# Four edits to a fused transformer kernel: early projections, interleaved scores, dealt experts, one-hots by half rows

## The chip, the cores and the metric

The kernel runs on one core of one Trainium2 chip. The metric is device time in microseconds, from the first to the last instruction of the program on that core. A core has TensorE (matmuls, into PSUM), VectorE, ScalarE and GpSimd (elementwise work), and SyncE, which here only issues DMAs. Each engine runs its own list of instructions in the order in which the kernel wrote it; they meet at semaphores. GpSimd can't read PSUM.

## The reference, cut to what matters

Input x is 4 batches of 512 tokens with 128 features, all float32. Between the parts the tokens are layer-normed.

```python
# layer 0, attention: gated, in groups of 32 tokens, plus a linear term over the batch
normed = layernorm(x)
v, gate = split(silu(normed @ W_h + b_h))          # 256 + 256
qk = silu(normed @ W_qk + b_qk)
quad_q, lin_q, quad_k, lin_k = qk * os_gamma[h] + os_beta[h]      # four scaled copies (as named there)
attn = relu(quad_q @ quad_k.T / 32 + bias) ** 2     # inside groups of 32
out = (gate * (attn @ v + lin_q @ (lin_k.T @ v) / n)) @ W_out + b_out + x
# layer 0, feed-forward: 8 experts of 128x128, the best 2 of them for each token
out = sum(top_w * (x @ We[top_idx]))
# layer 1, attention: 16 heads of 8, softmax features of q and k (16 each), causal
q, k = [softmax(p), softmax(-p)] of the mapped q and k
y = (q * cumsum(k v)) / (q * cumsum(k));  out = y @ w_out.T
# layer 1, feed-forward ("peer"): 8 heads; each token scores 2 x 32 keys a head, takes the best 8 of the
# sums, and mixes 64 of 1024 small experts: sum of sigmoid(score) * gelu(x . down[n]) * up[n]
```

## The kernel before, in words

Tokens stand in tiles of 128 (T = 4 a batch, 16 in all). The program has two parts, `layers` and `peer`.

**`layers`** runs rounds s = 1 to 4. In round s the batch a = s goes through layer 0 (helpers `a_...`) while the batch b = s - 1 goes through layer 1's attention (helpers `b_...`); batch 0's layer 0 stands ahead of the loop, and in round 4 there is only a `b`. Each engine has its own list, written by hand, in its own `for s in range(1, B + 1)` loop. In a round TensorE first projects batch a (`a_val`, `a_qk`, `a_gate`: 128x512 f32 matmuls from `wh` and `wqk`), between them it transposes tiles 2 and 3 of batch b and projects them (`b_x2t(b, 1)`, `b_qkv(b, 1)`); ScalarE takes the silu of queries, gates and values (L365, L383, L389), and the exponentials of layer 1's features (`b_exp`, L443). A change between silu and exp costs a table load. VectorE makes the maxima, sums and quotients of the features (`b_maps`, `b_features` L875 to L877), and GpSimd some scaled copies and differences.

The scores of layer 1 are `b_scores` (L1329): for each tile u and each group g of heads (four groups, each in 32 rows of the array) 8 matmuls of 32 rows and 128 columns, f16, high and low part of the query. A group's scores fill one PSUM bank (banks 4 and 5 in turn; in round 4 four banks), VectorE multiplies them with the causal mask (`b_masked`, L905) and sets the bank free, ScalarE and GpSimd split the product in f16 parts, and `b_numerators` (L1346 to L1363) multiplies them with the values into bank 6 or 7, where `b_summed` (L937) adds them up. Between these stand the experts of batch a: `a_experts` on TensorE (L1250, two matmuls of 128x512 f32 for a tile, each recorded as two instructions) and on VectorE (L842, 8 weighted sums a tile, two tiles in turn).

**`peer`** works on 8 pairs of tiles. Each token of a pair has chosen 64 experts, and their numbers are split in a high part (0 to 7) and a low part (0 to 127). For each pair, choices lie on 128 partitions: 64 of the first tile, 64 of the second; the 128 tokens of a tile are "lanes" on the free axis. `one_hots(p)` on VectorE writes `hot_hi` (L1876: is the high part e?), `hot_w` (L1882: that times the weight, in an f16 high and low part), and `hot_lo` (L1889: is the low part k? for three quarters of the lanes). ScalarE writes the last quarter, `hot_last` (L1746 for each lane, and L1752). `hot_w` has a block for each tile of the pair, and the block of the other tile is zero (a memset at the start, L1677). `gathered(p, q)` on TensorE (L2015) then takes each lane: the low one-hot (128x128) as weights, `hot_w` (16 columns: 2 tiles x 8) as moving data, twice (high and low part), so that both tiles of the pair lie beside each other in PSUM bank 2 + q. `weigh(p)` (L1904) multiplies that with the activations `hid` into `mix`, and scales by 1/4096. `outputs(p)` (L2029) multiplies `mix` with `upw`. Between these TensorE computes key scores for tiles two pairs ahead (`key_scores`, L1968) and the activations of the next batch (`hidden`, L1979; in pairs 2 to 5), and VectorE chooses the best keys (`first_choice` L1815, L1819; `second_choice` L1826, L1829). VectorE's order in a pair: one-hots, statistics of the pair before, second choice, `which_side`, `weigh`, first choice.

## Time and profile before

| | |
|---|---|
| median of 3 timed runs | 570.6 us (570.55 to 571.2) |
| the profiled execution's own time | 572.47 us |
| its span | 570.7 us |
| mean granted TensorE clock | 0.733 |
| busy: VectorE, TensorE, ScalarE, GpSimd | 481.5, 419.4, 307.2, 182.2 us |

The profiled execution is one execution of the program; its span runs from the first to the last recorded instruction. Its rows carry the start (us from the span's start), the length, the engine (PE is TensorE, PEld its weight load, DVE VectorE, ACT ScalarE, POOL GpSimd), the line of the kernel, the operation, and the tiles it writes and reads. In brackets stands for how long the engine had been idle and whom it waited for. `layers` takes the first 314 us or so, its rounds begin at about 67, 130, 192 and 256 us; pair 0 of `peer` writes its one-hots at about 345.

### The profile page before, as it was taken

What the parts mean: (1) busy time and instruction counts of PE and PEld (TensorE: products, weight loads), DVE (VectorE), ACT (ScalarE), POOL (GpSimd) and SP (SyncE); (2) the same over time, 40 slices, a digit from 0 to 9 for tenths busy, and PEclk for the clock granted to TensorE, in tenths of its full rate; (3) what the DMA queues carried; (4) which work ended last, traced back from release to release, by engine and by line L of the source; (5) the groups of instructions that cost most, each with busy time, mean ns of one, the idle gap of its engine ahead of it and who ended that gap; (6) DMA issues with size and microseconds to landing.
All of it is one profiled execution on the core that took longest, in us unless ns stands there. A gap on an engine that the chain in (4) does not pass through costs nothing. (4 is left out here: it accounts for less than half of the span.)

```text
span 570.7 us, 12499 instructions
## 1 busy us (share of the span) xinstructions
PE 419.4 (73%) x4564; PEld 300.4 (53%) x4564; DVE 481.5 (84%) x2076; ACT 307.2 (54%) x639; POOL 182.2 (32%) x208
## 2 busy tenths in 40 slices
PE   1777869987999879965754864756698869784485
PEld 1454547654776457633653323554465555554475
DVE  4485877699887989599894699999999999999991
ACT  0611275426652475313640558483788778786591
POOL 4540122943277143833350330303040404030000
PEclk9997979688867977795555785575757575757577
DMA  7220000000000000000000000000000000000000
GB/s 214 71 59 0 1 2 2 1 2 0 1 1 3 0 2 1 2 1 0 1 2 1 1 1 1 3 1 11 2 11 1 12 2 12 1 11 2 11 2 20
DMA packets 12459, 6.72 MB, mean 12 GB/s; under 512 B 3182, under 2 KB 11758, under 8 KB 12398
## 3 DMA queue, kind: packets, MB, share of 16 engines
q1 hardware_dynamic: 10566, 4.34, 2.8%
q10 hardware_dynamic: 1832, 1.58, 0.9%
q8 instruction: 36, 0.59, 0.4%
q14 instruction: 25, 0.20, 0.1%
HBM read 4.87 MB, written 1.05 MB: 10 GB/s over the span
## 5 line engine op out<-in xcount | busy, mean ns | idle before, releaser
L1746 ACT ACTIVATE hot_last<-iota_f,lo_last 128x128 f16<-128x128 f32 x256 | 77.5, 393 | 0.3 <-DVE lo_last L1872 0.3
L2015 PE MATMUL psum<-hot_w,hot_lo 128*128 128x16 f16 x1536 | 44.3, 174 | 25.1 <-DVE hot_lo L1889 17.9
L2015 PEld LDWEIGHTS psum<-hot_w,hot_lo 128*128 128x128 f16 x1536 | 43.4, 104 | 36.8 <-DVE hot_lo L1889 24.5
L1979 PE MATMUL psum<-x3t,down_t 128*128 128x512 f32 x64 | 45.3, 832 | 16.8 <-ACT hid L1711 15.1
L1889 DVE TENSOR_TENSOR hot_lo<-lo_t,iota_lo 128x4096 f16<-128x4096 f16 x24 | 53.6, 2287 | 0.3
L1659 POOL TENSOR_TENSOR eq<-eq,side_f 128x1024 f16<-128x1024 f16 x14 | 28.9, 2085 | 55.9 <-DVE eq L1850 55.9
L1329 PE MATMUL psum<-q_hi,k_t 32*128 32x128 f16 x256 | 36.1, 259 | 8.9 <-DVE masked L905 7.7
L1667 POOL TENSOR_TENSOR rstd<-rstd,minus_half 128x2 f32<-128x2 f32 x8 | 5.6, 702 | 113.4 <-DVE rstd L1922 113.4
L1819 DVE FIND_INDEX8 side_i<-side,keysims 128x8 uint32<-128x32 f32 x256 | 41.5, 184 | 0.0
L1250 PE MATMUL psum<-we,x1t 128*128 128x512 f32 x64 | 40.2, 777 | 0.4 <-DVE z L842 0.4
L2029 PE MATMUL psum<-upw,mix 128*128 128x128 f32 x256 | 36.9, 306 | 0.0
L584 POOL TENSOR_TENSOR a_rstd<-a_rstd,minus_half 128x2 f32<-128x2 f32 (+1 forms) x12 | 9.6, 803 | 84.6 <-DVE a_rstd L749 84.6
L1329 PE MATMUL psum<-q_lo,k_t 32*128 32x128 f16 x256 | 36.3, 261 | 0.0
L2029 PEld LDWEIGHTS psum<-upw,mix 128*128 128x128 f32 x256 | 36.3, 226 | 0.0
L636 POOL TENSOR_TENSOR s_lo<-masked,s_hi 128x512 f16<-128x512 f32 x28 | 31.7, 1157 | 12.4 <-ACT s_hi L472 8.7
L636 POOL TENSOR_TENSOR s_lo<-feat,s_hi 128x512 f16<-128x512 f32 x28 | 31.6, 1155 | 6.5 <-ACT s_hi L472 6.5
L1968 PE MATMUL psum<-keysim,xn 128*128 128x512 f32 x32 | 30.6, 1056 | 3.4 <-ACT keysims L1704 3.4
L1979 PEld LDWEIGHTS psum<-x3t,down_t 128*128 128x128 f32 x64 | 15.0, 256 | 33.9 <-ACT hid L1711 18.4
L1329 PEld LDWEIGHTS psum<-q_hi,k_t 32*128 32x128 f16 x256 | 24.4, 113 | 15.9 <-DVE masked L905 10.2
L472 ACT CAST s_hi<-masked 128x512 f16<-128x512 f32 x32 | 19.1, 617 | 23.5 <-DVE masked L905 23.5
L905 DVE TENSOR_TENSOR masked<-psum,causal 128x512 f32<-128x512 f32 x32 | 20.4, 683 | 11.7 <-PE psum L1329 11.5
L842 DVE SCALAR_TENSOR_TENSOR z<-psum,wexp,z 128x128 f32<-128x128 f32 x112 | 29.6, 341 | 0.0
(271 smaller groups left out, 1166.8 us busy)
## 6 DMA issues: line engine op xcount, KB each, us to landing
xall<-in_L_attn_x SPq DMA_DIRECT2D x4, 256.0 KB, 6.3
out<-o SPq DMA_DIRECT2D x8, 128.0 KB, 2.3
we<-in_L_ffn_We SPq DMA_DIRECT2D x1, 512.0 KB, 4.4
downn<-in_L_ffn_down SPq DMA_DIRECT2D x1, 512.0 KB, 5.3
upw<-in_L_ffn_up SPq DMA_DIRECT2D x1, 512.0 KB, 6.3
wh<-in_L_attn_W_h SPq DMA_DIRECT2D x1, 256.0 KB, 4.7
keysn<-in_L_ffn_keys_p ACTq DMA_DIRECT2D x1, 256.0 KB, 9.7
wqkv<-in_L_attn_w_qkv ACTq DMA_DIRECT2D x1, 192.0 KB
```

The source lines that it names most:

```text
L636: nc.gpsimd.tensor_tensor(s_lo[:, u % 2, g, :], masked[u % 2][:, g, :], s_hi[:, u % 2, g, :], ALU.subtract).then_inc(slo_ok.h, 1)
L842: ins = nc.vector.scalar_tensor_tensor(z2[:, u, :], src, wexp[:, u, e:e + 1], (z2 if e else x1)[:, u, :], ALU.mult, ALU.add)
L1250: ins = nc.tensor.matmul(bank[Y_BANK[u] + k][:], x1t[:, P * u:P * u + P], v.we[:, 4 * k:4 * k + 4, :].rearrange("p e m -> p (e m)"), start ...
L1329: ins = nc.tensor.matmul(bank[S_BANK[b][g]][:, P * c:P * c + P], k_t[r, u, c, :], q[r, u, c, :], start=(q is q_hi), stop=(q is q_lo))
L1659: nc.gpsimd.tensor_tensor(hit, hit, bc(side_f[:, u % 4].rearrange("p i r h -> p (i r) h").unsqueeze(3), [P, 2 * K, NH, K]), ALU.mult)\
L1746: ins = nc.scalar.activation(hot_last[:, lane], iota_f[:], ACT.Abs, bias=lo_last[:, lane:lane + 1], scale=-1.0)
L1819: ins = nc.vector.max_index(side_i[:, u % 4, s, :], side[:, u % 4, s, :], keysims[:, u % 4, s, :])
L1889: nc.vector.tensor_tensor(hot_lo[:, pairs], bc(lo_t[:, lanes].rearrange("p (j s) -> p j s", s=2).unsqueeze(2), [P, LB // 2, P, 2]), bc(v.i ...
L1968: nc.tensor.matmul(bank[6][:], xn[:, P * (u % T):P * (u % T) + P], v.keysim[:].rearrange("p s k -> p (s k)"), start=True, stop=True)\
L1979: nc.tensor.matmul(bank[H_BANK(b, c)][:], v.down_t[:, c, :], v.x3t[:, N * b:N * b + N], start=True, stop=True).then_inc(h_mm.h, 1)
L2015: ins = nc.tensor.matmul(bank[2 + q][:, c:c + 2 * EH], low, hot_w[:, i, lane // 2, :, :, lane % 2].rearrange("p t e -> p (t e)"), start=(i ...
L2029: ins = nc.tensor.matmul(outputs_of(p, t), mix[:, EH * t + e, :], v.upw[:, e, :], start=False, stop=(e == EH - 1))
```

## The change

Five things are moved or rewritten.

1. The projections of batch a (`a_qk`, `a_gate`, `a_val`) leave the start of round s and stand at the end of round s - 1 (the first ahead of the loop), on TensorE and ScalarE. With them some calls of the round change places: on VectorE the statistics `b_z3_spread` go ahead of `b_features(b, 0)`, `b_low_keys` and `a_attn` ahead of `b_x3`; on GpSimd the two head copies go ahead of a root.
2. `b_scores` computes the groups of a half in turn (as many as there are banks), one matmul of each, and waits for all their banks first.
3. The expert matmuls of tile 1 are dealt between the scores of tiles 2 and 3; the numerators of tile 1 come after those scores. On VectorE the first expert sums go ahead of `b_summed(b, 1)`.
4. `hot_w` has no zero block any more. It is written in two products on all 128 partitions, and `gathered` multiplies the two halves of the partitions separately: 4 matmuls a lane, of 64 rows and 8 columns, the two tiles into two banks. `weigh` is a plain product; the scale goes into `upw`, once, on GpSimd.
5. In `peer` the first key scores stand ahead of the second `hidden`.

```diff
 ScalarE
+                def a_front(b):
+                    a_qk(b)
+                    a_gate(b, 0)
+                    a_val(b, 0)
+                    a_val(b, 1)
+                    a_gate(b, 1)
...
                 act.wait_ge(pads.h, 2)
+                a_front(1)
                 for s in range(1, B + 1):
                     a, b = s, s - 1
                     b_exp(b, 0)
                     b_x2t(b, 1)
                     if a < B:
-                        a_qk(a)
                         a_heads(a)
                     b_maps(b, 1)
-                    b_features(b, 0)
-                    if a < B:
-                        a_val(a, 0)
-                        a_gate(a, 0)
-                        a_val(a, 1)
-                        a_gate(a, 1)
-                    b_exp(b, 1)
                     b_values(b, 1)
                     if a < B:
                         a_link(a)
+                    b_features(b, 0)
                     b_value_head(b)
-                    if b > 0:
-                        b_x3t(b - 1)
+                    b_exp(b, 1)
                     if a < B:
                         a_kv(a)
                     b_value_part(b)
                     b_transposed(b, 0)
+                    if b > 0:
+                        b_x3t(b - 1)
...
                     b_yt(b)
+                    if a + 1 < B:
+                        a_front(a + 1)
 VectorE
-                    b_features(b, 0)
                     if b > 0:
                         b_z3_spread(b - 1)
+                    b_features(b, 0)
                     b_maps(b, 1)
+                    b_low_keys(b, 0)
+                    if a < B:
+                        a_attn(a)
                     if b > 0:
                         b_x3(b - 1)
-                    if a < B:
-                        a_attn(a)
-                    b_low_keys(b, 0)
...
                         b_masked(b, 3)
+                        a_experts(a, 0)
                         b_summed(b, 1)
-                        a_experts(a, 0)
 TensorE
                     for s in range(1, B + 1): ...
-                    if a < B:
-                        a_val(a, 0)
-                        a_qk(a)
-                        a_gate(a, 0)
                     b_x2t(b, 1)
                     if a < B:
-                        a_val(a, 1)
+                        a_link(a)
                     b_qkv(b, 1)
                     if a < B:
-                        a_gate(a, 1)
                         a_sim(a)
-                        a_link(a)
+                        a_kv(a)
+                    b_transposes(b, 0)
+                    if a < B:
+                        a_outt(a, 0)
                     if b > 0:
                         b_x3t(b - 1)
-                    if a < B:
-                        a_kv(a)
-                        a_outt(a, 0)
-                    b_transposes(b, 0)
...
                         b_numerators(b, 0)
                         a_experts(a, 0)
-                        a_experts(a, 1)
                         b_scores(b, 2, (1,))
+                        a_experts(a, 1, (0,))
                         b_scores(b, 3, (0,))
+                        a_experts(a, 1, (1,))
+                        b_scores(b, 3, (1,))
                         b_numerators(b, 1)
-                        b_scores(b, 3, (1,))
                         b_numerators(b, 2)
...
+                    b_yt(b)
+                    if a + 1 < B:
+                        a_qk(a + 1)
                     b_z3(b)
+                    if a + 1 < B:
+                        a_rest(a + 1)          # gate 0, val 0, val 1, gate 1
 b_scores
-                    for g in (2 * i + j for i in halves for j in range(2)):
-                        banks = len(set(S_BANK[b]))
-                        if 4 * u + g >= banks:
-                            wait(pe, masked_ok, b, 4 * u + g - banks + 1)
-                        r = slice(32 * g, 32 * g + 32)
+                    for first in range(0, len(groups), banks):
+                        together = groups[first:first + banks]
+                        if 4 * u + together[-1] >= banks:
+                            wait(pe, masked_ok, b, 4 * u + together[-1] - banks + 1)
                         for c in range(QUADS):
                             for q in (q_hi, q_lo):
+                                for g in together: ...
 peer
-                nc.gpsimd.memset(hot_w[:], 0.0).then_inc(zeroed.h, 1)
...
+                nc.gpsimd.tensor_scalar(v.upw[:], v.upw[:], 1.0 / WEIGHT_SCALE, None, ALU.mult).then_inc(upw_ok.h, 1)
...
-                    for t in range(2):
-                        q = slice(HK * t, HK * t + HK)
-                        for i, w in enumerate((w_hi, w_lo)):
-                            ins = nc.vector.tensor_tensor(
-                                hot_w[q, i, :, t], hot_hi[q],
-                                bc(w[q].rearrange("p (j s) -> p j s", s=2).unsqueeze(2), [HK, P // 2, EH, 2]),
-                                ALU.mult)
+                    for i, w in enumerate((w_hi, w_lo)):
+                        ins = nc.vector.tensor_tensor(
+                            hot_w[:, i], hot_hi[:],
+                            bc(w[:].rearrange("p (j s) -> p j s", s=2).unsqueeze(2), [P, P // 2, EH, 2]), ALU.mult)
...
-                        wait(dve, g_mm, p, q + 1)
+                        wait(dve, g_mm, p, q // 2 * 2 + 2)
...
                         for i in range(2):
-                            c = 2 * EH * (lane % LB)
-                            ins = nc.tensor.matmul(
-                                bank[2 + q][:, c:c + 2 * EH], low,
-                                hot_w[:, i, lane // 2, :, :, lane % 2].rearrange("p t e -> p (t e)"),
-                                start=(i == 0), stop=(i == 1))
+                            for t in range(2):
+                                half, c = slice(HK * t, HK * t + HK), EH * (lane % (2 * LB))
+                                low = hot_lo[half, lane // 2, :, lane % 2] if q < QB - 1 else hot_last[half, lane - LB * q, :]
+                                ins = nc.tensor.matmul(
+                                    bank[2 + q // 2 * 2 + t][:, c:c + EH], low, hot_w[half, i, lane // 2, :, lane % 2],
+                                    start=(lane % (2 * LB) == 0 and i == 0), stop=(i == 1), skip_group_check=True)
...
                 hidden(0, 0)
+                key_scores(0)
                 hidden(0, 1)
-                key_scores(0)
```

## Rows read from the trace of the kernel before

**Rows 1.** The page, busy us, share of the span and instructions of each engine.
```profile
PE 419.4 (73%) x4564; PEld 300.4 (53%) x4564; DVE 481.5 (84%) x2076; ACT 307.2 (54%) x639; POOL 182.2 (32%) x208
```
**Rows 2.** Windows: stretch, its length, PE, PEld, DVE, ACT, POOL busy, clock, DMA.
```profile
455.00:490.00 35.00, 29.53 (x365) 22.07 (x364) 34.51 (x241) 24.38 (x58) 7.54 (x12) 0.63 0.02 6
```
**Rows 3.** The chain that ended last, pair 4 of the last layer: start, us, what.
```profile
461.88 0.61 DVE hot_hi L1876
462.51 1.28 DVE hot_w L1882 x2
...
479.90 2.39 DVE mix L1904 x4
...
491.14 0.61 DVE hot_hi L1876
```
**Rows 4.** VectorE's waits from 95 to 250: for whom, us, times, longest.
```profile
DVE masked L905 <- PE psum L1329: 11.5, 3, 4.2
```
**Rows 5.** Timeline around 170 us, round 2: start, us, engine, line, operation.
```profile
168.08 4.82 PE L1250 MATMUL psum<-we,x1t 128*128 128x512 f32 x8
...
173.55 0.69 DVE L905 TENSOR_TENSOR masked<-psum,causal 128x512 f32<-128x512 f32 x1 [3.43 <-PE psum L1329]
```
**Rows 6.** Groups by line: shapes, count, busy us, mean ns, idle before.
```profile
L905 DVE TENSOR_TENSOR masked<-psum,causal 128x512 f32<-128x512 f32 x32 | 20.4, 683 | 11.7 <-PE psum L1329 11.5
...
L1882 DVE TENSOR_TENSOR hot_w<-hot_hi,w_hi 64x1024 f16<-64x1024 f16 x16 | 11.0, 685 | 0.4
L1882 DVE TENSOR_TENSOR hot_w<-hot_hi,w_lo 64x1024 f16<-64x1024 f16 x16 | 10.9, 679 | 0.0
...
L1876 DVE TENSOR_TENSOR hot_hi<-hi_t,iota_hi 128x1024 f16<-128x1024 f16 x8 | 5.5, 684 | 0.0
```
**Rows 7.** Timeline of VectorE in the last pair.
```profile
559.23 0.69 DVE L1904 SCALAR_TENSOR_TENSOR mix<-psum,hid 128x512 f32<-128x512 f32 x1 [2.08 <-PE psum L2015]
```
**Rows 8.** Timelines of TensorE and VectorE in pair 2.
```profile
420.03 1.86 PE L2015 MATMUL psum<-hot_w,hot_last 128*128 128x16 f16 x64
...
421.28 2.48 DVE L1904 SCALAR_TENSOR_TENSOR mix<-psum,hid 128x512 f32<-128x512 f32 x4
```
**Rows 9.** Timeline of TensorE in pair 4.
```profile
467.94 1.90 PE L2015 MATMUL psum<-hot_w,hot_lo 128*128 128x16 f16 x64
...
475.00 2.06 PE L1968 MATMUL psum<-keysim,xn 128*128 128x512 f32 x2
477.17 1.86 PE L2015 MATMUL psum<-hot_w,hot_last 128*128 128x16 f16 x64
```
**Rows 10.** Timeline of TensorE, scores of groups 0 and 1 in round 1.
```profile
93.31 0.23 PE L1329 MATMUL psum<-q_hi,k_t 32*128 32x128 f16 x1
...
93.54 0.23 PE L1329 MATMUL psum<-q_hi,k_t 32*128 32x128 f16 x2
...
93.95 0.21 PE L1329 MATMUL psum<-q_lo,k_t 32*128 32x128 f16 x1
```
**Rows 11.** Timeline at the start of the last layer.
```profile
314.67 3.75 PE L1979 MATMUL psum<-x3t,down_t 128*128 128x512 f32 x4 [1.68 <-PEq L316]
...
316.47 0.81 ACT L1696 ACTIVATE xn<-x3t,bn_shift,bn_scale 128x512 f32<-128x512 f32 x1 [1.13 <-DVE bn_shift L1935]
...
318.22 1.06 PE L1968 MATMUL psum<-keysim,xn 128*128 128x512 f32 x1
```
**Rows 12.** Groups by line, GpSimd.
```profile
L605 POOL TENSOR_SCALAR heads_t<-qk_t,gam,bet 128x512 f32<-128x512 f32 x8 | 7.7, 968 | 0.1
```
**Rows 13.** Timeline at the start of round 2.
```profile
131.66 1.02 PE L1155 MATMUL psum<-x3t,wh 128*128 128x512 f32 x2
...
132.97 1.06 ACT L443 ACTIVATE pe_in<-pe_in 128x1024 f32<-128x1024 f32 x1 [4.97 <-DVE pe_in L867]
...
134.06 1.22 DVE L875 TENSOR_REDUCE psum_<-pe_in 128x128 f32<-128x1024 f32 x1
...
141.56 1.28 ACT L443 ACT_TABLE_LOAD   x1
```
**Rows 14.** Timeline of VectorE, first query split of round 1.
```profile
87.49 0.69 DVE L893 SCALAR_TENSOR_TENSOR q_lo<-psum,q_hi 128x512 f16<-128x512 f32 x1 [3.00 <-ACT q_hi L463]
```

More of the change, by code:

```diff
@@ L1241, in a_logits, with a_experts @@
                     ins.then_inc(logit_mm.h, 1)
-                def a_experts(b, u):
+                def a_experts(b, u, halves=(0, 1)):
                     if u == 2 and b:
@@ L1248, in a_experts @@
                         wait(pe, y_used, b, 1)
-                    for k in range(2):
+                    for k in halves:
                         ins = nc.tensor.matmul(bank[Y_BANK[u] + k][:], x1t[:, P * u:P * u + P],
@@ L1321, in b_scores @@
                         wait(pe, qlo_ok, b, 3)
-                    for g in (2 * i + j for i in halves for j in range(2)):
-                        banks = len(set(S_BANK[b]))
-                        if 4 * u + g >= banks:
-                            wait(pe, masked_ok, b, 4 * u + g - banks + 1)
-                        r = slice(32 * g, 32 * g + 32)
+                    banks = len(set(S_BANK[b]))
+                    groups = [2 * i + j for i in halves for j in range(2)]
+                    for first in range(0, len(groups), banks):
+                        together = groups[first:first + banks]
+                        if 4 * u + together[-1] >= banks:
+                            wait(pe, masked_ok, b, 4 * u + together[-1] - banks + 1)
                         for c in range(QUADS):
                             for q in (q_hi, q_lo):
-                                ins = nc.tensor.matmul(bank[S_BANK[b][g]][:, P * c:P * c + P], k_t[r, u, c, :],
-                                                       q[r, u, c, :], start=(q is q_hi), stop=(q is q_lo))
-                        ins.then_inc(a_mm.h, 1)
+                                for g in together:
+                                    r = slice(32 * g, 32 * g + 32)
+                                    ins = nc.tensor.matmul(bank[S_BANK[b][g]][:, P * c:P * c + P], k_t[r, u, c, :],
+                                                           q[r, u, c, :], start=(q is q_hi), stop=(q is q_lo))
+                                    if c == QUADS - 1 and q is q_lo:
+                                        ins.then_inc(a_mm.h, 1)
                 def b_numerators(b, u):
@@ L1373, in b_z3 @@
                     ins.then_inc(yt_mm.h, 1)
+                def b_z3(b):
                     wait(pe, yt_ok, b)
@@ L1903, in weigh @@
                         lanes = slice(LB * q, LB * q + LB)
[L1904 to L1907 removed]
+                        columns = slice(EH * LB * (q % 2), EH * LB * (q % 2 + 1))
+                        nc.vector.tensor_tensor(
+                            mix[:].rearrange("p (t e) l -> p t e l", t=2)[:, :, :, lanes],
+                            v.psum[:, 2 + q // 2 * 2:4 + q // 2 * 2, columns].rearrange("p t (l e) -> p t e l", e=EH),
+                            hid[:, b % 2, at:at + 2, :, lanes], ALU.mult).then_inc(mix_ok.h, 1)
                 def residual(p):
@@ L2007, in gathered @@
                     if p:
-                        wait(pe, mix_ok, p - 1, q + 1)
+                        wait(pe, mix_ok, p - 1, q // 2 * 2 + 2)
                     elif q == 0:
```

31 lines of the change are left out of this document (18 added, 13 removed).

## The prediction

> **What bounds the kernel now.** I read first the busy line and the windows, then the chain that ended last, then the timelines of one pair and of one round. VectorE is busy 481.5 of 570.7 us [rows 1], and in the stretch from 455 to 490 us 34.5 of 35.0 [rows 2]: the last layer is VectorE. The chain there runs through VectorE alone, from one pair's one-hots to the next pair's, 29.3 us apart (461.88 to 491.14), and four `hot_w` products stand in it, 1.28 us for each two [rows 3]. TensorE's work hides under it, with little room. In the rounds before (the attention and expert layers of two batches side by side, about 62 us each) VectorE waits at few places: the largest is for scores, 11.5 us in three waits [rows 4], one of which is the 3.43 us at 173.55, while TensorE spends 4.82 us on the experts of two tiles [rows 5].
>
> **One-hots by half rows.** Four products on 64 partitions become two on 128. A product's time hangs on its free size: 64x1024 takes 679 to 685 ns, and `hot_hi`, which is 128x1024, takes 684 [rows 6]. So each pair loses two of four, 1.28 us on the chain [rows 3]. Over pairs 0 to 6: 9.0 us. The last pair gains nothing: its last mix waits 2.08 us for its last gather [rows 7]; that gather needs ScalarE's one-hots, and these start from `lo_last`, ahead of the products on VectorE. The mixing itself (four scaled products of 128x512 from PSUM, 2.39 us on the chain [rows 3]) becomes plain products of the same size; the mask product from PSUM takes 683 ns [rows 6], two of them about 1.2. I take nothing for it; the bounds are 0.1 us either way per pair. It now waits for two quarters at a time. In the last pair two mixes stand behind the last gather instead of one: +0.6. In pair 2 the last gather started at 420.03 and took 1.86, and the mixes began at 421.28 [rows 8]; 1.29 earlier, the third would want to start at 421.2, and must wait for 421.9: 0.8 of the gain is lost there. In pair 4 the third mix comes at 479.90 - 1.29 + 1.20 = 479.8, and the last gather ends at 479.03 [rows 9]: 0.8 us of room, no wait.
>
> The price is TensorE's. A quarter is 64 matmuls of 16 columns, about 1.85 us, 29 ns each [rows 9]. It becomes 128 matmuls of 8 columns on 64 rows, alternating between the halves of the array. Nothing in the trace has this form. Lower bound: the halves run side by side, 1.85 us a quarter. Upper bound: each matmul costs its own slot, 3.7 us. The nearest rows are the score matmuls on 32 rows: one group of rows alone starts one every 55 ns, but where the second group's begin (93.54) two start in the same time, and 16 that would need 0.88 us one by one start within 0.64 [rows 10]. That shows two row groups working side by side, with their weight loads, so I take the lower bound plus a little, 14 to 16 ns each, which the 0.8 us of room in pair 4 just holds. What the rows don't show is whether instructions of this shortness are handed out fast enough: the gap there was 27 ns on average, and here 14 is needed.
>
> Against this stands a rule of the Trainium skill, page "TensorEngine Tiling (Array Packing)", section "Performance Considerations": a matmul has an overhead of some 60 cycles, so one column costs as much as sixty, and one shouldn't take a tiling factor from a dimension that is already small. By that rule 8 columns cost what 16 did and the gathers double. It is the first rival below.
>
> **Start of the last layer.** The first key scores move ahead of one pair of hidden matmuls. Now they start at 318.22, behind 3.75 us of four matmuls, though their input was ready at 316.47 + 0.81 = 317.28 [rows 11]. They start then at 317.3: -0.9 us, and VectorE's first choice follows. The scaling of `upw` on GpSimd (128x1024) replaces a longer memset; GpSimd's multiply and add on 128x512 take 0.97 [rows 12], so about 1.9, behind the first candidates and long before the first gather that waits for it. Nothing; without that cover, 1.9 once.
> Last layer: -9.0 + 0.8 + 0.6 - 0.9 = **-8.5 us**.
>
> **Experts dealt between the scores.** The second half of tile 2's scores stands now behind one tile's experts instead of two: 2.4 us of 4.82 less [rows 5]. The rest of tile 1's experts falls between scores that wait for masks anyway. The scores of two head groups in turn give both banks some 0.2 to 0.4 us sooner (0.64 instead of 0.88, or more where one group waited for its own mask); against this the next pair must wait for both masks. VectorE has other work between halves, so I take 0.4 us a round, bounds -0.5 to +1. Given back: numerators of tile 1 come later, VectorE's first expert sums (about 4.2 us) stand ahead of their summing, and the numerators of tile 3 wait for that bank: 0.6 us more of VectorE's work before the last expert sums and 0.2 of waiting, 0.8. Net -2.0 in each of three rounds: **-6.0 us**. In the last round four groups in turn halve TensorE's time, but VectorE is what they wait for there: 0.
>
> **Next batch's values, gates, queries a round early.** TensorE does the same f32 matmuls at the same place, behind VectorE's last expert sum (4.5 us ahead of 134.06), only without a tile's transposes between: gate, two values, gate, each about 1.0 to 1.2 us (one at 131.66 is 1.02 [rows 13]), ending some 4.5 us after VectorE's last expert sum. ScalarE now has five activations of them, and the table load, in front of the first exponentials of the round, so these wait: the last gate ends at +5.3, a table load of 1.28, the exponentials 1.06 [rows 13]: +7.6, where VectorE, with the z3 statistics moved ahead, would be ready at +6.0. Before it got them at once, at +4.5 (134.06 [rows 13]). So a stall of 1.6 us is new in rounds 2 and 3. What it buys: the values are there when the similarities want them, so links, transposes and gated products are ready early, and some 2.6 us of short waits between 149 and 156 us shrink; but a_out still follows VectorE. I take 0.7 back: +0.95 in rounds 2 and 3, together +1.9. Round 1 has a wait of 3.00 us ahead of its first query split [rows 14] and smaller ones of some 1.9 before; they absorb a stall of 3: -1.9. On SP's queue nothing is moved. On GpSimd two head products move ahead of a root whose reader comes later. Together 0.
> Layers: -6.0 + 1.9 - 1.9 = **-6.0 us**.
>
> **Sum.** -8.5 - 6.0 = -14.5. The profiled execution took 572.47 with a span of 570.7, the runs 570.6 in the median; the difference is taken from the median: **556 us**.
>
> **The rivals.**
> (A) *Gathers double* (ends slower). Each short matmul costs the old slot, 27 to 29 ns. In pair 4 TensorE works without a break from 467.94 [rows 9]: 3.7 + 1.85 + 7.4 + 2.05 + 3.6 = 18.6, so the last gather ends at 486.5 and the third mix, due at 479.8, waits 6.7: net +5.4 in each of four pairs with hidden matmuls, +0.5 in pairs 0 and 1, -0.8 in pair 6, +3.4 in the last: about +25, with the layers and the first scores +18: 588. If the fuller array holds its clock (key scores take 2.06 at the lower clock [rows 9], half at the higher), 3 us of each such pair come back: 576. I take 582. It decides from about 16 ns a matmul, and turns the whole slower from about 22. For it: no row shows such matmuls closer than 27 ns; against it: the overlap in [rows 10].
> (B) *Half way*, 18 to 20 ns: a wait of 2 to 2.5 us in four pairs: 564.
> (C) *The front is cold.* Where TensorE stands at the lower clock, the moved block takes 9 us instead of 4.5, and the first exponentials wait 6 us in rounds 2 and 3, 3 more in round 1: 556 + 11 = 567. For it: a mean granted clock of 0.63 from 455 to 490 us [rows 2]; against: two f32 matmuls of 512 columns took 1.02 there [rows 13], which is the 2.4 GHz level, where 2.06 [rows 9] is the 1.2 GHz one.
>
> **How the numbers follow.** Forecast 0.54, A 0.25, B 0.13, C 0.08. 0.2% is what a measurement can tell, 569.5 to 571.7. Faster: forecast, B, most of C, less a remainder for layer terms that go wrong: 0.70; slower: A, 0.25; same 0.05. The forecast's own range is 549 to 563 (layers -10 to 0, mixing and masks 2); with B, C and the better half of A: 549 to 582.
>
> **What would show it.** Right: `hot_w` x16 at 128x1024 and 11 us busy in place of 22; a quarter of 128 matmuls in 2.0 us or less; pairs about 28.0 us apart; no wait of a mix on a gather but in pairs 2 and 7; the wait of `masked` for scores near 1 us instead of 3.4 to 4.2; a new wait of `psum_` for the exponentials of 1 to 2 us at a round's start. Wrong: a mix that waits 2 us or more in pairs 2 to 5 (A or B), a round longer than 62 us (C, or the expert sums given back in full).

## The result, and the profile after

The changed kernel took 574.57 us in the median of 17 runs (573.38 to 578.78), the kernel before, run beside it, 570.93 (569.92 to 573.71). The ratio is 1.006, with a 95% interval of 1.004 to 1.007: slower by 3.3 us by that ratio (3.6 between the medians), where 14.6 us less were forecast. The time lies outside the forecast's own range (549 to 563). It lies inside the wide one (549 to 582), but that was drawn for rivals A, B and C; that the time falls into it is luck, since what happened is none of the three as they were told.

The page of the changed kernel: busy us, share of the span and instructions of each engine, for [rows 1].

```profile
PE 403.2 (70%) x6612; PEld 281.2 (49%) x6612; DVE 476.9 (83%) x2060; ACT 309.0 (54%) x639; POOL 181.2 (32%) x208
```

VectorE has 4.6 us less to do, although its products with the weights alone lost 10.9 (below): something else that it does became some 6 us longer. TensorE has 2048 matmuls more, each with its weight load. Split at the first pair's one-hots, the trace says where the time went: the stretch before them grew from 345.2 to 348.9 us, the stretch from there to the end shrank only from 225.5 to 224.8.

**The last layer.** Groups by line, for [rows 6]:

```profile
L1908 DVE TENSOR_TENSOR hot_w<-hot_hi,w_hi 128x1024 f16<-128x1024 f16 x8 | 5.5, 692 | 0.3
L1908 DVE TENSOR_TENSOR hot_w<-hot_hi,w_lo 128x1024 f16<-128x1024 f16 x8 | 5.5, 684 | 0.0
...
L911 DVE TENSOR_TENSOR masked<-psum,causal 128x512 f32<-128x512 f32 x32 | 20.4, 683 | 6.0 <-PE psum L1348 5.7
...
L1930 DVE TENSOR_TENSOR mix<-psum,hid 128x512 f32<-128x512 f32 x32 | 20.3, 683 | 11.5 <-PE psum L2043 11.5
```

The products cost what was foreseen: 11.0 us busy instead of 21.9, and a pair's one-hots take 9.1 us instead of 10.5. But `mix` now waits 11.5 us for TensorE: 2.3, 1.0, 0.7 and 1.1 us in pairs 2 to 5, 0.3 and 6.1 in pair 7. The chain that ended last, in pair 4, for [rows 3] (start, us, what):

```profile
473.42 2.28 PE psum L2043 x164
475.70 0.99 issue
476.70 1.39 PE psum L2043 x70
478.09 2.00 PE psum L1994 x2
480.09 1.82 PE psum L2043 x128
481.91 0.02 issue
481.94 1.29 DVE mix L1930 x2
```

Before, this chain ran through VectorE alone in pair 4. Now it runs through TensorE, and it holds a piece called "issue": 0.99 us in which TensorE waits for nothing that the profile shows. The timeline of TensorE in the last pair has such pieces too (start, us, engine, line, operation, count, and in brackets the idle time before and its cause):

```profile
548.46 3.16 PE L2043 MATMUL psum<-hot_w,hot_lo 64*128 64x8 f16 x233
553.00 1.86 PE L2043 MATMUL psum<-hot_w,hot_lo 64*128 64x8 f16 x127 [1.38 <-issue]
556.54 0.49 PE L2043 MATMUL psum<-hot_w,hot_lo 64*128 64x8 f16 x24 [1.69 <-issue]
556.87 1.55 PE L2043 MATMUL psum<-hot_w,hot_last 64*128 64x8 f16 x104
560.37 0.48 PE L2043 MATMUL psum<-hot_w,hot_last 64*128 64x8 f16 x24 [1.96 <-issue]
```

127 matmuls in 1.86 us are 14.6 ns each (13.4 from one start to the next), inside the forecast's 14 to 16. Then comes a pause, about once in 128 matmuls, which are 256 instructions with their weight loads. The last gather of this pair ends 17.7 us after its one-hots began (543.2 to 560.9), before it was 15.3 (543.9 to 559.2), and the third mix waits 6.1 us.

**The layers.** VectorE's waits from 60 to 300 us (for whom, us in total, times, longest), for [rows 4]:

```profile
DVE psum_ L881 <- ACT pe_in L452: 10.0, 3, 7.3
DVE masked L911 <- PE psum L1348: 5.7, 3, 2.4
DVE q_lo L899 <- ACT q_hi L472: 3.5, 6, 1.1
```

The last of these before:

```profile
DVE q_lo L893 <- ACT q_hi L463: 10.0, 11, 3.0
```

The wait for scores halved, as forecast for the dealt experts. The wait for query splits (`q_lo`) was 10.0 us and is 3.5, as forecast for the early values. A wait for the exponentials came in their place: 1.3 us in rounds 2 and 3 (1.6 was forecast), 7.3 us in round 1 (3 was forecast). In rounds 2 and 3 TensorE begins the moved block of projections 1.4 us before VectorE's last expert sum ends and takes 5.8 us for it, at a granted clock of 1.00, the 2.4 GHz level (from 130.8 and from 194.7 us). In round 1 it begins 1.7 us after that sum and takes 6.7 us (from 68.1): from 68.4 to 71.8 the granted clock was 0.50, the 1.2 GHz level. The exponentials therefore start 10.5 us after that sum instead of 6.5. Why the block begins late in round 1 is open. The waits add up to less than before, and yet the layers are 4.4 us longer. So VectorE's own instructions must have grown somewhere. Cutting the rounds at VectorE's instructions shows where to look (us; each a difference of two starts or ends in its timeline; `a_z`, L793, adds batch a's attention output to its input, and the expert sums come after it):

| | before | after | e2 front | e9 | e10 |
|---|---|---|---|---|---|
| round 1, last expert sum to `a_z` | 27.4 | 31.3 | 31.2 | 28.7 | 26.0 |
| round 2 | 26.2 | 28.6 | 28.0 | 27.1 | 29.6 |
| round 3 | 27.6 | 27.8 | 28.1 | 27.1 | 29.6 |
| round 4, last expert sum to first mask | 22.5 | 24.1 | 24.1 | 22.5 | 24.1 |
| rounds 1 to 3, `a_z` to the experts, sum | 71.4 | 64.9 | 74.5 | 62.9 | 66.5 |

The dealt part is 6.5 us shorter and gives 0.8 us back in each of three rounds (first to second expert sums 8.9 instead of 8.1 us): -4.2. The starts are 8.2 us longer in all. How far can such a table be trusted? Four kernels below (e1, e5, e6, e7) leave the layers as they were; in their traces the starts of rounds 1 to 3 add up to 79.2 to 81.4 us (before 81.1, changed 87.7), and the first one-hots come at 343.1 to 345.9 us (before 345.2, changed 348.9). So one or two microseconds between two columns say nothing, and 6 to 8 do.

In round 2 of the changed kernel, VectorE's timeline, and under it GpSimd's:

```profile
146.42 1.76 DVE L892 SCALAR_TENSOR_TENSOR k<-feat,k 128x256 f16<-128x256 f32 x2
148.11 0.68 DVE L776 SCALAR_TENSOR_TENSOR sim<-psum,bias_t 128x512 f32<-128x512 f32 x1
148.82 1.65 DVE L779 SCALAR_TENSOR_TENSOR attn_t<-sim 128x512 f32<-128x512 f32 x1
```

```profile
146.57 1.34 POOL L626 TENSOR_TENSOR vrest<-values,vparts 128x512 f32<-128x512 f32 x1 [0.61 <-ACT vparts L445]
148.72 1.20 POOL L630 TENSOR_TENSOR vparts<-vrest,vparts 128x512 bf16<-128x512 f32 x1 [0.82 <-ACT vparts L466]
```

And the same operations of the kernel before:

```profile
143.85 0.69 DVE L773 SCALAR_TENSOR_TENSOR attn_t<-sim 128x512 f32<-128x512 f32 x1
144.46 0.75 DVE L886 SCALAR_TENSOR_TENSOR k<-feat,k 128x256 f16<-128x256 f32 x2
```

```profile
145.35 1.20 POOL L620 TENSOR_TENSOR vrest<-values,vparts 128x512 f32<-128x512 f32 x1 [2.21 <-ACT vparts L436]
```

`attn_t` took 0.69 us and takes 1.65; the two `k` took 0.75 together and take 1.76. Before, the subtraction began when both were done. Each of the long ones ends shortly after a GpSimd subtraction that ran over it (146.57 + 1.34 = 147.91, and `sim` begins at 148.11; 148.72 + 1.20 = 149.92). The page of the Trainium skill "SBUF — State Buffer", section "SBUF: two separate sides", has a rule for this: a VectorE operation with two SBUF inputs and a GpSimd operation that reads SBUF share one pair of ports, whichever starts first holds it for its whole length, and the other fully blocks. The rows agree: `attn_t` and the second `k`, which read SBUF twice, lose 0.96 and 1.01 us (`sim`, between them, ran while GpSimd stood still and tests nothing). The mask product `masked`, which reads PSUM and SBUF once each, takes 683 ns on average in the 24 cases in which it lies over a GpSimd product for more than 0.3 us, and 685 in the other 8. Over the whole changed kernel four `k` are 1.00 us longer each, three `attn_t` 0.95, and one `x` (L760, in round 4: 1.30 us where the others take 0.34) 0.97: together 7.8 us. Before, of these three only `x` met GpSimd (its head copies), for 1.2 us.

### The profile page after: what moved, and what is told of

It is laid out like the page before. It is cut to its first block and busy times, and to the rows that moved or that the text cites. A ratio compares the mean times of both kernels' runs of the same rounds, so it can differ in the third digit from the quotient of the medians.

```text
span 573.7 us, 16580 instructions
## 1 busy us (share of the span) xinstructions
PE 403.2 (70%) x6612; PEld 281.2 (49%) x6612; DVE 476.9 (83%) x2060; ACT 309.0 (54%) x639; POOL 181.2 (32%) x208
## 5 line engine op out<-in xcount | busy, mean ns | idle before, releaser
L2043 PE MATMUL psum<-hot_w,hot_lo 64*128 64x8 f16 x3072 | 45.2, 164 | 29.2 <-issue 20.4
L2043 PEld LDWEIGHTS psum<-hot_w,hot_lo 64*128 64x128 f16 x3072 | 42.9, 100 | 42.4 <-issue 29.1
L2005 PE MATMUL psum<-x3t,down_t 128*128 128x512 f32 x64 | 44.1, 812 | 16.1 <-ACT hid L1739 14.5
L1348 PE MATMUL psum<-q_hi,k_t 32*128 32x128 f16 x256 | 20.2, 257 | 20.7 <-DVE masked L911 14.3
L1930 DVE TENSOR_TENSOR mix<-psum,hid 128x512 f32<-128x512 f32 x32 | 20.3, 683 | 11.5 <-PE psum L2043 11.5
L848 DVE SCALAR_TENSOR_TENSOR z<-psum,wexp,z 128x128 f32<-128x128 f32 x112 | 29.6, 340 | 0.0
L1780 ACT ACTIVATE hot_last<-hot_last 128x4096 f16<-128x4096 f16 x8 | 28.9, 3617 | 0.3
L1732 ACT COPY keysims<-psum 128x512 f32<-128x512 f32 x16 | 9.8, 612 | 34.8 <-PE psum L1994 34.8
```

The costliest lines, as they stand in the source:

```text
L848: ins = nc.vector.scalar_tensor_tensor(z2[:, u, :], src, wexp[:, u, e:e + 1], (z2 if e else x1)[:, u, :], ALU.mult, ALU.add)
L1930: nc.vector.tensor_tensor(mix[:].rearrange("p (t e) l -> p t e l", t=2)[:, :, :, lanes], v.psum[:, 2 + q // 2 * 2:4 + q // 2 * 2, columns] ...
L2005: nc.tensor.matmul(bank[H_BANK(b, c)][:], v.down_t[:, c, :], v.x3t[:, N * b:N * b + N], start=True, stop=True).then_inc(h_mm.h, 1)
L2043: ins = nc.tensor.matmul(bank[2 + q // 2 * 2 + t][:, c:c + EH], low, hot_w[half, i, lane // 2, :, lane % 2], start=(lane % (2 * LB) == 0 a ...
```

## The experiments

Two theories stood after the traces. *Supply*: TensorE's instructions arrive in blocks, and the short matmuls outrun them. *Collision*: the new order at a round's start lets GpSimd block VectorE. Beside them stood *queue*: ScalarE's front stands ahead of the exponentials.

### Parts of the change alone: e1, e2, e3, e4

Their edits are items of the change, and nothing else. e1 has only item 4, the half rows:

```diff
-        hot_w = sb("hot_w", [P, 2, P // 2, 2, EH, 2], F16)
+        hot_w = sb("hot_w", [P, 2, P // 2, EH, 2], F16)
...
+                            for t in range(2):
+                                half, c = slice(HK * t, HK * t + HK), EH * (lane % (2 * LB))
```

> The kernel before with one edit of the change alone: the one-hot products by half rows (hot_w without its zero half, 128 gather matmuls of 64 rows by 8 columns a quarter instead of 64 of 128 by 16, the mix of both tables, the scale put into upw). Supply theory (mine, from the changed kernel's trace: gather matmuls start 13.4 ns apart, but about once in 256 instructions TensorE stands still for 0.8 to 2.1 us with nothing to wait for, so it is fed no faster than some 256 instructions in 3.4 to 3.7 us): VectorE's one-hots fall from 10.5 to 9.1 us a pair, mix waits some 1.2 us a pair longer for TensorE, and the total is 569.5 to 571 (0 to -1 us). Rival (the last layer's gain of 8 us is real, and something in the changed layers delays it): 562 to 564. Rival 2 (GpSimd's scaling of upw or the start of the last layer costs it): as slow or slower than 573, with the loss before the first pair.

Measured: 571.62 us, ratio 1.000 [0.998, 1.002]; 225.4 us from the first one-hots to the end, against 225.5. Of 9 us of VectorE's products nothing is left, and nothing in the layers is to blame. The time lies 0.6 us above the supply theory's range; beside its own runs of the kernel before (571.75) it is 0 to -1 us, as that theory said.

e2 has only item 1, the front, with the orders that go with it on four engines:

```diff
+                a_front(1)
                 for s in range(1, B + 1):
...
-                    b_low_keys(b, 0)
                     b_features(b, 1)
```

> The kernel before with the next batch's values, gates and queries made at the end of a round, and the orders of ScalarE, VectorE and TensorE at the start of a round that go with it; nothing else of the change. My theory: the starts of the rounds (last expert sum to a_z) cost +4.0, +2.5, +0.2 and +1.6 us as in the changed kernel, so 577 to 580 (+6.5 to +8.5). Rival (the losses at the starts come from the dealt experts or the interleaved scores, which leave TensorE's work elsewhere): 566 to 571. Nothing in the last layer moves by over 0.5 us.

Measured: 582.71 us, ratio 1.018 [1.013, 1.022], +10 us. Slower than my theory said. The starts add 7.7 us (table), with the same long `k`, `attn_t` and `x` as in the changed kernel, and the stretch from `a_z` to the experts adds 3.1, which I had not expected. The rival is out.

e3 has only items 2, 3 and 5, the interleaved scores, the dealt experts and the early key scores:

```diff
-                        a_experts(a, 1)
                         b_scores(b, 2, (1,))
+                        a_experts(a, 1, (0,))
                         b_scores(b, 3, (0,))
+                        a_experts(a, 1, (1,))
```

> The kernel before with the experts dealt between the scores, the scores of two head groups in turn, and the key scores of the first tile ahead of the second hidden product; no front, no half-row one-hots. My theory (the dealt section of the changed kernel was 2.5, 1.2 and 2.8 us shorter in rounds 1 to 3 and 0.8 was given back after each, the key scores gave 0.7): 565 to 567 (-4 to -5.5). Rival (the section is only shorter in the changed kernel because its front had been moved out of it): 569 to 571.

Measured: 569.07 us, ratio 0.996 [0.995, 0.997], -2.3 us: faster, but half of what my theory said, and inside the rival's range. Its trace has the dealt stretches 6.0 us shorter, 2.3 given back, and starts 1.6 longer, most of which is inside the spread of traces with equal layers. The rival's reason, that the section is only shorter where the front had been moved out of it, is not borne out: it is 6.0 us shorter here without the front.

e4 has items 1, 2 and 3: the changed kernel without half rows and early key scores, the diffs of e2 and e3.

> The changed kernel without its half-row one-hots and without the key scores moved: front, dealt experts and interleaved scores. My theory (last b_y 4.4 us later in the changed kernel, its last layer no shorter for the one-hots than 0.7 us): 574.5 to 576, as slow as the changed kernel plus 1 us. Rival (the one-hots do bring their 8 us, and the layers cost 12): 581 to 583.

Measured: 577.03 us, ratio 1.009 [1.008, 1.011]. Above my theory's range by 1 us, 4 us under the rival's. From e1 to e4 the parts don't quite add: e2 and e3 give +8, e4 has +5.4, perhaps because the dealt experts shorten just the stretch that the front lengthens (argued, not tested).

### Is it the supply of instructions? e5, e6, e7

The page has a row for the queue that brings instructions. Before, and after:

```profile
q8 instruction: 36, 0.59, 0.4%
```

```profile
q8 instruction: 52, 0.85, 0.6%
```

16 packets more, for 2 x 2048 = 4096 more instructions of TensorE: 256 instructions and 16 KB a packet. Three kernels change how fast TensorE goes through them. e5 leaves out the products with the weights' low part, so its result is rounded more coarsely:

```diff
-                        for i in range(2):
+                        for i in range(1):
                             for t in range(2):
```

> The half-row kernel of the first experiment, with the products of the low part of the weights left out (64 matmuls of 64 rows by 8 columns a quarter, 128 instructions with their weight loads, as many as the kernel before issues; the weights are then rounded to half precision). Supply theory (TensorE is fed some 256 instructions in 3.35 us when it outruns its feed): the quarters come 2.2 us apart by hot_lo, 128 instructions each, which is under that rate, so the pauses inside quarters go, each quarter takes 0.9 to 1.0 us, mix waits for nothing but hot_last, and the total is 560 to 564. Rival (a pause belongs to the matmuls by half rows, one in about 128 of them): a pause of 1.1 to 1.9 us still falls in every second quarter, and the total is 566 to 569.

Measured: 561.82 us, ratio 0.983 [0.981, 0.986]; 216.9 us from the first one-hots to the end, 8.6 less than before. TensorE's timeline in pair 4:

```profile
461.13 1.02 PE L2018 MATMUL psum<-hot_w,hot_lo 64*128 64x8 f16 x64
462.53 2.08 PE L1980 MATMUL psum<-x3t,down_t 128*128 128x512 f32 x2 [0.38 <-ACT hid L1714]
464.54 1.87 PE L2018 MATMUL psum<-hot_w,hot_lo 64*128 64x8 f16 x128
```

Same form of matmul, same pace, 128 in a row, no pause inside a quarter, and `mix` waits once, for 3.2 us, in the last pair. The pause is not a property of the half rows. (Before the last quarter TensorE stands 1.6 to 3.6 us, also called "issue": there it waits for ScalarE's one-hots.)

e6 and e7 issue each gather matmul twice, by half rows and by full rows. e6 doesn't compute the kernel's result: in every second quarter its second pass adds to the first. Each ran once.

```diff
-                    for lane in range(LB * q, LB * q + LB):
+                    for lane in 2 * list(range(LB * q, LB * q + LB)):
```

> The half-row kernel of the first experiment with every gather matmul issued twice (256 a quarter, 512 instructions; the sums of every second quarter come out doubled). Supply theory: a quarter is fed in two blocks of 256 at 3.35 us, so 6.5 to 7.5 us a quarter, 13.1 ns an instruction, with two pauses of about 1.5 us in each; the last layer takes 60 to 90 us longer. Rival (the pauses come from waiting on hot_lo or PSUM, not from the feed): 3.7 to 4.5 us a quarter, 26 matmuls of 13.4 ns after one another without a pause.

> The kernel before with every gather matmul (128 rows by 16 columns) issued twice: 128 matmuls and 256 instructions a quarter, as many as the changed kernel. Supply theory: a matmul takes 28 to 29 ns here, so 256 instructions take 3.7 us, just slower than the feed of 3.35 us: no pause over 0.3 us inside a quarter, 3.7 us a quarter. Rival (a pause of 1.1 to 1.9 us for each 256 instructions whatever their pace): 4.8 to 5.6 us a quarter.

e6: 685.96 us. The timeline of TensorE, two quarters of a pair in a row:

```profile
487.05 1.87 PE L2018 MATMUL psum<-hot_w,hot_lo 64*128 64x8 f16 x128 [0.16 <-issue]
490.78 1.86 PE L2018 MATMUL psum<-hot_w,hot_lo 64*128 64x8 f16 x127 [1.86 <-issue]
494.88 1.87 PE L2018 MATMUL psum<-hot_w,hot_lo 64*128 64x8 f16 x128 [2.23 <-issue]
498.60 0.46 PE L2018 MATMUL psum<-hot_w,hot_lo 64*128 64x8 f16 x23 [1.86 <-issue]
```

128 matmuls, a pause, 128 matmuls, a pause: a block of 256 instructions every 3.7 to 4.1 us, and 32 packets more on the instruction queue (84) for 8192 more instructions. The layer became 116 us longer where I had said 60 to 90: the sustained supply is slower than the 3.35 us that I had taken from pair 4. 3.7 to 4.1 us for 128 matmuls are 29 to 32 ns each, which is rival A's price, by way of pauses.

e7: 599.16 us. Its timeline:

```profile
486.67 7.02 PE L2015 MATMUL psum<-hot_w,hot_lo 128*128 128x16 f16 x256
```

The same number of gather instructions as the changed kernel, the same 52 packets, and not one pause in 512 instructions: 27.4 ns a matmul, 3.5 us a block. No other gather of this trace has one over 0.3 us either, but for the wait before the layer's first, which every kernel has. So a pause does not come with every 256 instructions; it comes where they are used up in 1.87 us.

The pauses go with the rate of instructions, not with the form or number of matmuls. The trace also keeps the start and length of each packet of the instruction queue, and they tie the pauses to it. The last pair of the changed kernel (us):

| packet starts | has come in | pause ends | after the packet |
|---|---|---|---|
| 550.42 | 551.44 | 553.00 | 1.56 |
| 554.13 | 555.03 | 556.54 | 1.51 |
| 557.77 | 559.03 | 560.37 | 1.34 |

All 17 "issue" pauses of over 0.5 us before or inside its gathers (the layer's first gather apart) end 1.2 to 1.6 us after a packet has come in; in e6 all 46 do. The pauses before the last quarter in e5, which wait for ScalarE, end 2.2 to 4.1 us after one. And no two packets start less than 3.2 us apart in any of the traces, e6's included, where TensorE stood waiting for them. **Shown:** TensorE waits for its next 256 instructions. **Open:** why the next packet isn't asked for sooner.

### e8: half rows only where the supply holds

Quarters 0 and 1 by half rows, 2 and 3 by full rows, on e3. The weights' two parts lie side by side, so one product makes both:

```diff
-                        for i, w in enumerate((w_hi, w_lo)):
...
+                    J = P // 4
+                    w2 = w_both[:].rearrange("p j i s -> p j (i s)").unsqueeze(2)
+                    nc.vector.tensor_tensor(
+                        hot_w[:].rearrange("p j e i s -> p (j e) i s"),
...
                     for t in range(2):
                         q = slice(HK * t, HK * t + HK)
...
+                        ins = nc.vector.tensor_tensor(
+                            hot_v[q, :, t].rearrange("p j e i s -> p j (e i s)"),
```

> The third experiment's kernel (dealt experts, interleaved scores, key scores first) with half rows in quarters 0 and 1 of a pair and full rows in quarters 2 and 3: 768 instructions of the gather a pair (512 before, 1024 in the changed kernel), and the products with the weights in three VectorE instructions of 1024 elements instead of four. Supply theory: VectorE is 0.64 us a pair shorter, the feed needs 10 us from quarter 0's start to quarter 3's end, which is inside the 11.1 us it has, so mix comes no later: 564 to 566, 3 to 5 us below the third experiment. Rival (any half-row quarter makes its pause and the mix wait for it): 568 to 570.

Measured: 565.08 us, ratio 0.989 [0.987, 0.991], 4 us under e3. Its `mix` waits for TensorE:

```profile
DVE mix L1926 <- PE psum L2042: 2.7, 2, 2.4
```

768 instructions a pair instead of 1024 leave one pause of 0.8 us in pair 4 and no wait there; the two waits are in pairs 2 (0.3 us) and 7 (2.4). `hot_w` serves quarters 0 and 1, `hot_v`, which has the zero block again, quarters 2 and 3.

### Why the rounds start late: e9, e10, e11

e9 makes GpSimd wait; no work changes:

```diff
                         wait(pool, v1_ok, b)
+                        if b:
+                            wait(pool, x3_ok, b - 1)
+                        else:
+                            wait(pool, attn_ok, 1)
                         nc.gpsimd.tensor_tensor(vrest[:], values[:], vparts[:, :, :, 0, 0:HD], ALU.subtract)
```

> The changed kernel with one wait more: GpSimd's two subtractions for the value parts of a round wait until VectorE is through with low_keys, attn and x3. Contention theory (in the changed kernel a low_keys instruction takes 1.42 us instead of 0.42, attn_t 1.64 instead of about 0.75, and in round 4 an x3 instruction 1.30 instead of 0.34, each while a subtraction runs on GpSimd; in the kernel before none of them falls together with one): these fall back to 0.42, 0.75 and 0.34 us, each round starts 1.5 to 1.9 us sooner, total 567 to 570 (-4.5 to -7.5 against the changed kernel's 574.6). Rival (VectorE waits there for TensorE or ScalarE anyway): the instructions get short, the time stays at 573.5 to 575.5. Rival 2 (the value parts come too late for the first products): later than 576.

Measured: 568.18 us, ratio 0.995 [0.992, 0.997], 1.1% under the changed kernel: a wait added, 6 us gained. Round 2, VectorE:

```profile
143.14 0.75 DVE L896 SCALAR_TENSOR_TENSOR k<-feat,k 128x256 f16<-128x256 f32 x2
143.81 0.68 DVE L780 SCALAR_TENSOR_TENSOR sim<-psum,bias_t 128x512 f32<-128x512 f32 x1
144.53 0.69 DVE L783 SCALAR_TENSOR_TENSOR attn_t<-sim 128x512 f32<-128x512 f32 x1
```

`k` and `attn_t` are back at 0.75 and 0.69, the four starts are 6.4 us shorter, VectorE's busy time is 7.3 us less (469.6 instead of 476.9), and round 4 starts in 22.5 us as in the kernel before. On GpSimd the subtractions now run beside VectorE's features:

```profile
146.39 1.20 POOL L630 TENSOR_TENSOR vrest<-values,vparts 128x512 f32<-128x512 f32 x1 [3.72 <-DVE x L764]
148.41 2.29 POOL L634 TENSOR_TENSOR vparts<-vrest,vparts 128x512 bf16<-128x512 f32 x1 [0.82 <-ACT vparts L466]
```

The first keeps its 1.20 us and so do the features; the second takes 2.29 instead of 1.20, so here it is GpSimd that is held, and it has the time.

e10 moves ScalarE's part of the front behind the exponentials:

```diff
-                a_front(1)
                 for s in range(1, B + 1):
                     a, b = s, s - 1
                     b_exp(b, 0)
+                    if a < B:
+                        a_front(a)
                     b_x2t(b, 1)
...
                     b_yt(b)
-                    if a + 1 < B:
-                        a_front(a + 1)
```

> The changed kernel with ScalarE's part of the front (queries, gates, values of the next batch, some 4.5 to 5 us) put behind b_exp(b, 0) of the round instead of before it; TensorE's part stays early. Queue theory (b_exp(b, 0) stands behind the front in ScalarE's order: in round 1 features(0) starts 11.6 us after VectorE's last expert sum, before 4.9): features(0) starts 2.5 to 4 us sooner in round 1 and 1 to 2.5 us in rounds 2 and 3, but the copy x2t(b, 1) and with it maps(1) stays where it was, behind the same 5 us, so about half comes back: total 570.5 to 573. Rival (ScalarE's order is not what starts the round late): 574 to 576.

Measured: 571.21 us, ratio 1.000 [0.997, 1.002]; 0.6% under the changed kernel. Its ten executions lie between 569.7 and 575.8, and the profiled one, 575.07, is among the slowest, so what follows is read from a slow example. What the queue theory forecast came: the first features start 6.7 us sooner after the last expert sum in round 1 (2.5 to 4 forecast) and 1.7 us sooner in rounds 2 and 3 (1 to 2.5). But up to `a_z` only round 1 gains, 5.3 us; rounds 2 and 3 lose 1.0 and 1.8. The wait moved:

```profile
DVE pmin L870 <- ACT pm L431: 7.8, 4, 3.6
```

Before, the exponentials were late (10.0 us of waits for them in the changed kernel, 0.7 here), and now the copy `x2t` is, and `maps(1)` with it.

e11 has both edits, the diffs of e9 and e10.

> Both edits of the two runs before in one kernel. If the two causes are separate, the gains add: 563 to 569. If features(0) sooner only moves VectorE's work into the same wait, the time is that of the better one alone, within 1 us.

Measured: 567.83 us, ratio 0.993 [0.990, 0.996]. It can't be told from e9; the last `b_y` starts at 297.3 instead of 298.5 us. Both forecasts contain this time; but e9 gained 6.4 us on the changed kernel and e10 3.4, and both together 6.7, so the gains don't add. The collision was most of it.

### e12: all of it, repaired

The changed kernel with the diffs of e8, e9 and e10.

> The changed kernel with its three losses repaired: half rows in quarters 0 and 1 only (as in e8), the value parts of GpSimd behind VectorE's low_keys, attn and x3 (e9), ScalarE's part of the front behind b_exp(b, 0) (e10). It differs from e8 by the repaired front alone. If the early front is worth nothing once its losses are gone (the last b_y is at 297.3 us in e11 and at 297.3 us in e8): 563.5 to 566, the same as e8's 565.1 within the measurement. If it brings what the prediction's first-round term had hoped (2 us) and more: 560 to 563.

Measured: 563.49 us, ratio 0.986 [0.984, 0.989]. It beats the kernel before by 1.4% and the changed kernel by 1.9%. Its interval overlaps e8's (which ran beside other runs of the kernel before), so whether the repaired front is worth anything is open.

## Why the prediction was wrong, step by step

- **One-hots, VectorE's part: right.** 685 ns on 128 partitions (684 to 692 measured), the mix at its old size (683), 1.4 us a pair. Where no `mix` waits, in pairs 0 and 1, the next one-hots come after 26.9 and 27.9 us instead of 28.3 and 29.3.
- **One-hots, TensorE's part: the first step that failed.** "I take the lower bound plus a little, 14 to 16 ns each." The pace of matmuls that have arrived is just that, 14.6 ns. The prediction named the right doubt, "whether instructions of this shortness are handed out fast enough", and gave it no price. The page of the kernel before has the packets (36, 0.59 MB, so 16 KB each), and the count would go up by 4096 instructions; how fast packets can follow one another, no row before shows. Rival A had the right direction and the wrong mechanism: it asked for 27 ns a matmul; the measured case is 14.6 ns and a pause of 0.5 to 2 us where a block runs out; `mix` waits six times, 11.5 us in all, and that eats the 10.9 that the shorter products gave. Rival B, 18 to 20 ns a matmul, has no such pace in the rows either. The last layer, -8.5 said with the key scores, is 0.7 us shorter from the first one-hots on. e5 gained 8.6 us from the first one-hots on; the forecast for that stretch was 9.0 - 0.8 - 0.6 = 7.6. That bears out VectorE's terms. It doesn't show that the whole sum would have held with a faster supply, because e5 has only half the gather matmuls, and so more room on TensorE than the forecast kernel.
- **Last pair: +0.6 said.** From its one-hots to the third mix 17.7 us where the last mix came after 15.3: +2.4.
- **Key scores first: the start right, the worth not.** -0.9 said. The first key scores start 14.8 us after the last `b_y` in all seven kernels with this edit and 15.7 in all seven without: 0.9. But the first one-hots, for which it was meant, come 42.0 to 43.0 us after `b_y` with it and 42.3 to 43.5 without, 42.6 and 42.7 on average. The 0.7 us between the changed kernel and the one before is inside that spread. The prediction followed VectorE's first choice and not what comes after it.
- **Dealt experts: mis-sized.** -6.0 said; -4.2 in the changed kernel's trace, about -2 by itself (e3). The 0.8 given back was right to the tenth (8.9 instead of 8.1).
- **Front: the second step that failed.** "Together 0" said; the starts alone +8.2. The exponentials were worked out rightly for rounds 2 and 3 (a stall of 1.3 us where 1.6 was said; round 1 waits 7.3 instead of 3). What was missed is in the list of calls that "change place" beside the front: `low_keys` and `attn` now meet GpSimd's subtractions. The prediction looked for what each call waits for, and never for what runs beside it; the term stands in its sum as nothing. The long instructions add up to 7.8 us against 1.2 before, and e9 prices them at 6 us of time, more than the whole slowdown.
- **Rival C (cold front): out in rounds 2 and 3, where the moved block ran at a granted clock of 1.00. In round 1 it holds in part:** the granted clock was 0.50 for 3.4 us of the block, and it took 6.7 us instead of 5.8.
- **A slip in the sum.** In pair 2 the third mix "would want to start at 421.2, and must wait for 421.9" makes 0.7 us lost, not 0.8. It changes nothing.

Taken together: -4.2 (deal), +8.2 (starts), +0.4 (start of round 1), -0.7 (last `b_y` to first one-hots) and -0.7 (last layer) are +3.0, the difference of the two spans (573.7 and 570.7). That is one pair of traces taken apart, and its terms under 2 us are inside what two executions differ by.

## What to carry to other kernels

When an edit splits matmuls into shorter ones, count TensorE's instructions beside their time: here 256 of them used up in 1.87 us ran dry again and again, 256 in 3.5 us did not, and packets of 256 never started less than 3.2 us apart. When calls change order, lay the new order of VectorE beside that of GpSimd, and look for operations with two inputs in SBUF that come to lie over GpSimd's; making GpSimd's work wait was worth 6 us here, more than the 4.2 that the dealt experts brought. And split a mixed change on the chip: one part of this one cost 10 us and another brought 2.

## What was not expected of the hardware

Matmuls of 64 rows by 8 columns, the two halves in turn, start every 13.4 ns on average while their instructions last, weight loads included (128 of 16 columns every 26.8). TensorE then pauses, 0.5 to 2.3 us in the changed kernel and e6, until 1.2 to 1.6 us after the next packet of 256 instructions has come in, and sustains 14.5 to 16 ns an instruction (e6). At 13.7 ns an instruction it did not pause in 512 (e7); a longer unbroken stretch at that pace was not run. The Trainium skill, page "TensorEngine Tiling (Array Packing)", section "Performance Considerations", would have had 8 columns cost as much as 16. The price of a lane did not double as that would have it: with two row halves in turn a matmul takes 14.6 ns against 27.4. Whether a half costs less by itself, or two halves lie side by side, no run here shows; none issued one half alone.

A VectorE instruction of 0.41 us took 1.42 beside a GpSimd subtraction, one of 0.69 took 1.65, and one of 0.34, which reads one large tile and two columns of scalars, took 1.30. No wait is shown for it: the instruction itself is longer.
